# Pairing the row maxima of two PSUM banks on VectorE, spreading the value products, and weighing one chunk earlier, in a two-layer decoder

## What is computed

```python
qh  = (q @ w_q).reshape(B, L, 16, 8).transpose(0, 2, 1, 3)   # 16 heads of 8
kvp = c @ w_kv                                   # c: 6404 context rows
k, v = kvp[..., :8], kvp[..., 8:]                # one key and value head for all
prob = softmax(einsum('bhid,bjd->bhij', qh, k) / sqrt(8))
out  = einsum('bhij,bjd->bhid', prob, v)...reshape(B, L, 128) @ w_concat
```

## Time and profile before

| | before |
|---|---|
| median of 3 runs | 2091.1 us |
| the profiled execution, its own time | 2089.03 us |
| its span | 2087.3 us |
| PE busy | 1963.3 us (94%) |
| DVE busy | 1571.0 us (75%) |
| ACT busy | 1360.1 us (65%) |
| POOL busy | 98.9 us (5%) |
| maxima of the first cross attention, L981 | 1664 reductions, 976.3 us busy |
| exponentials there, L965 | 1632 activations, 874.0 us busy |

### The profile page before, as it was taken

How to read it: one execution, slowest core, us unless ns; L and a number is a source line. 1 busy time by engine, 2 the same in 40 slices (tenths; PEclk the granted TensorE clock), 3 DMA queues, 4 the chain that set the end, 5 groups by cost and what they waited for, 6 DMA issues and landing times. The chain is left out here.

```text
span 2087.3 us, 38311 instructions
## 1 busy us (share of the span) xinstructions
PE 1963.3 (94%) x15036; PEld 1030.1 (49%) x15036; DVE 1571.0 (75%) x3006; ACT 1360.1 (65%) x2404; POOL 98.9 (5%) x84
## 2 busy tenths in 40 slices
PE   7778999999999999999999999898999988999898
PEld 2225744444444444444444444676344435777755
DVE  7995899999999999999999951333788854444344
ACT  5333488888888888888888887332588863333421
POOL 1660000000000000000000000001000000000000
PEclk8998899999999999999999999898999998999999
DMA  4210000000000000000000000110000000000011
GB/s 144 71 61 0 1 2 2 2 1 2 2 1 2 2 1 2 2 2 1 2 2 1 2 1 1 31 38 18 0 1 1 2 1 1 1 1 0 11 33 28
DMA packets 22853, 24.73 MB, mean 12 GB/s; under 512 B 5712, under 2 KB 20080, under 8 KB 22432
## 3 DMA queue, kind: packets, MB, share of 16 engines
q1 hardware_dynamic: 21504, 20.37, 3.3%
q10 hardware_dynamic: 1184, 2.10, 0.3%
HBM read 21.74 MB, written 0.59 MB: 11 GB/s over the span
## 5 line engine op out<-in xcount | busy, mean ns | idle before, releaser
L981 DVE TENSOR_REDUCE sb_max_partial<-ps_max_ps 128x1 f32<-128x512 f32 (+1 forms) x1664 | 976.3, 662 | 61.1 <-PE ps_max_ps L796 60.4
L965 ACT ACTIVATE sb_probs<-ps_score_ps 128x512 f32<-128x512 f32 (+1 forms) x1632 | 874.0, 597 | 111.0 <-PE ps_score_ps L929 65.6
L929 PE MATMUL ps_score_ps<-sb_q_stack,sb_key_stack 64*128 64x512 f32 x1632 | 586.6, 444 | 3.9 <-ACT sb_probs L965 3.4
L796 PE MATMUL ps_max_ps<-sb_key_stack,sb_q_stack 64*128 64x512 f32 (+1 forms) x1560 | 555.7, 438 | 0.0
L918 PE MATMUL ps_acc_ps<-sb_probs,sb_val_ones 128*32 128x256 f32 x6528 | 465.0, 387 | 0.2 <-ACT sb_probs L965 0.2
L929 PEld LDWEIGHTS ps_score_ps<-sb_q_stack,sb_key_stack 64*128 64x128 f32 x1632 | 276.8, 184 | 326.2 <-ACT sb_probs L965 267.9
L796 PEld LDWEIGHTS ps_max_ps<-sb_key_stack,sb_q_stack 64*128 64x128 f32 x1560 | 265.1, 184 | 9.6 <-DVE sb_max_partial L981 7.3
L918 PEld LDWEIGHTS ps_acc_ps<-sb_probs,sb_val_ones 128*32 128x32 f32 x6528 | 156.4, 108 | 207.0 <-issue 144.2
L1630 DVE TENSOR_REDUCE sb_s_max_partial<-ps_s_ps 128x1 f32<-128x512 f32 x256 | 159.9, 683 | 21.7 <-PE ps_s_ps L1539 21.6
L1617 ACT ACTIVATE sb_s_probs<-ps_s_ps 128x512 f32<-128x512 f32 x256 | 140.7, 597 | 25.6 <-PE ps_s_ps L1567 16.6
L1914 DVE TENSOR_SCALAR_CACHE_REDUCE sb_x_scores<-ps_x_score_ps 128x1024 f32<-128x1024 f32 (+1 forms) x56 | 62.1, 1111 | 82.4 <-PE ps_x_score_ps L1855 82.4
(11 more groups left out here) (269 smaller groups left out, 1827.7 us busy)
## 6 DMA issues: line engine op xcount, KB each, us to landing
sb_val<-c_rows SPq DMA_DIRECT2D x16, 512.0 KB, 3.7
sb_e_w<-L_ffn_rW SPq DMA_DIRECT2D x30, 128.0 KB, 2.1
sb_e_w<-L_ffn_W_T SPq DMA_DIRECT2D x24, 128.0 KB, 2.1
sb_ctx_T<-ctx_T SPq DMA_DIRECT2D x1, 1664.0 KB, 7.7
sb_ctx_T<-ctx_T ACTq DMA_DIRECT2D x1, 1538.0 KB, 8.7
sb_x_T<-x_T SPq DMA_DIRECT2D x1, 512.0 KB, 3.8
sb_x_tok<-x ACTq DMA_DIRECT2D x1, 512.0 KB, 11.1
sb_e_w<-L_ffn_sW SPq DMA_DIRECT2D x4, 128.0 KB, 2.4
```

Of the source, the lines that this page charges most:

```text
L796: nc.tensor.matmul(bank((blk, u))[:, 0:n], queries, keys, start=True, stop=True).then_inc(tile_ready, 1)
L929: nc.tensor.matmul(score_ps[:, e % 3, :], k.key_stack[rows(blk), c * P:(c + 1) * P], q_stack[rows(blk), blk // 2, j * HALF:(j + 1) * HALF] ...
L965: nc.scalar.activation(probs[0:n, c % 3, j * HALF:(j + 1) * HALF], score_ps[0:n, e % 3, :], ACT.Exp).then_inc(exp_done, 1)
L981: nc.vector.tensor_reduce(partial[:, blk % 2, h, r:r + 1], bank((blk, u))[:, 0:RANGES[r][1]], AX.X, ALU.max).then_inc(tile_used, 1)
```

## The change

There are four parts.

1. **Pairs.** Where two tiles that follow one another lie in the first and second bank of the ring (and both are full 512-key tiles of one head), VectorE reduces both with one instruction over 2 x 512 columns, `pair_maxima` (L998 of the changed kernel). It waits for the second tile, and frees both banks when it ends. All other tiles keep their own reduction.
2. **Values.** The 51 value products of layer 0 are no longer jobs. They are issued one at a time between the tiles of block 0, from tile 21 to tile 96, all into one PSUM bank, and ScalarE copies them at the end with two instructions in place of five. 27 jobs are left, spread over the same tiles. The queries of the upper half use one PSUM bank in place of two, and each waits for the one before.
3. **Chunk 49** (`NCH - 2`) is weighed at the end of its own block, ahead of the transposes of shift B, no longer behind score 0 of the next block. Chunk 50 stays behind score 0.
4. **Self attention.** Likewise chunk 6 (`NT - 2`) is weighed at its block's end, and chunk 7 behind score 1 of the next block in place of score 0; ScalarE copies the sum after exponential 1 in place of 0.

```diff
-            val0_jobs = [(c, min(13, NCH - 1 - c)) for c in range(0, NCH - 1, 13)] + [(NCH - 1, 1)]
...
+            def paired(blk, u):
+                return (u % NR < NR - 2 and place[(blk, u)] % PLACES in (0,)
+                        and place[(blk, u + 1)] == place[(blk, u)] + 1)
...
-                return score_ps[:, i % 2, :]
+                return score_ps[:, 0, :]
...
-                    pe.wait_ge(q_done, i - 3 if i < HB else i - 1)
+                    pe.wait_ge(q_done, i - 3 if i < HB else i)
...
+            def value(pe, c):
+
+                n = P if c < NCH - 1 else TAIL
+                ins = nc.tensor.matmul(v_ps[0:n, c, :], k.ctx_T[:, c * P:c * P + n], k.w_kv[:, HD:2 * HD], start=True,
+                                       stop=True)
+                if c == NCH - 1:
+                    ins.then_inc(v_ready, 1)
...
+            VALUE_AT = {FIRST_JOB + 1 + 3 * c // 2: c for c in range(NCH)}
...
                     if e == 0 and blk > 0:
-                        weigh(pe, blk - 1, NCH - 2)
                         weigh(pe, blk - 1, NCH - 1)
...
+                weigh(pe, blk, NCH - 2)
                 if blk + 1 < NB:
                     issue(pe, (blk + 1, "B"))
...
+            def pair_maxima(dve, blk, u):
+
+                h, r, at = u // NR, u % NR, place[(blk, u)] % PLACES
+                dve.wait_ge(tile_ready, blk * TILES + u + 2)
+                nc.vector.tensor_reduce(partial[:, blk % 2, h, r:r + 2], max_ps[:, at:at + 2, :],
+                                        AX.X, ALU.max).then_inc(tile_used, 2)
...
                         for u in range(TILES):
-                            maximum(dve, blk, u)
+                            if u > 0 and paired(blk, u - 1):
+                                pair_maxima(dve, blk, u - 1)
+                            elif not paired(blk, u):
+                                maximum(dve, blk, u)
...
-                    if e == 0 and blk > 0:
-                        weigh(pe, blk - 1, NT - 2)
+                    if e == 1 and blk > 0:
                         weigh(pe, blk - 1, NT - 1)
...
+                weigh(pe, blk, NT - 2)
```

More of the change, by code:

```diff
@@ L725, in context_attention @@
             job_ready, job_copied = k.sem("layer1_job_ready"), k.sem("layer1_job_copied")
+            v_ready, v_taken = k.sem("ctx_v_ready"), k.sem("ctx_v_taken")
             EXPS = NCH * JOBS
-            val0_jobs = [(c, min(13, NCH - 1 - c)) for c in range(0, NCH - 1, 13)] + [(NCH - 1, 1)]
             key_jobs = [(c0, min(HALF, CTX - c0)) for c0 in range(0, CTX, HALF)]
             val_jobs = [(c, min(4, NCH - 1 - c)) for c in range(0, NCH - 1, 4)] + [(NCH - 1, 1)]
-            VAL0, KEYS = len(val0_jobs), len(key_jobs)
-            NJOBS = VAL0 + KEYS + len(val_jobs)
+            KEYS = len(key_jobs)
+            NJOBS = KEYS + len(val_jobs)
             EARLY_JOBS = NJOBS
@@ L853, in job_bank, with take_values @@
                 return acc_ps[:] if i % 2 else score_ps[:, 2, :]
-            def layer1_job(pe, i, to):
[L857 to L864, removed]
+            v_ps = score_ps[:, 1, 0:NCH * HD].rearrange("p (c e) -> p c e", e=HD)
+            def value(pe, c):
[4 more added lines that the diff above has]
+                    ins.then_inc(v_ready, 1)
+            def take_values(act):
+                act.wait_ge(v_ready, 1)
+                nc.scalar.copy(k.val_ones[:, 0:NCH - 1, 0:HD], v_ps[:, 0:NCH - 1, :])
+                nc.scalar.copy(k.val_ones[0:TAIL, NCH - 1, 0:HD], v_ps[0:TAIL, NCH - 1, :]).then_inc(v_taken, 1)
+            def layer1_job(pe, i, to):
+                if i < KEYS:
+                    c0, cols = key_jobs[i]
                     ins = nc.tensor.matmul(to[:, 0:cols], k.wk1[:], k.ctx_T[:, c0:c0 + cols], start=True, stop=True)
                 else:
-                    c, m = val_jobs[i - VAL0 - KEYS]
+                    c, m = val_jobs[i - KEYS]
                     n = P if c < NCH - 1 else TAIL
@@ L1013, in _ @@
                             subtract_high(pe, MINUS_AT[u])
+                        if u in VALUE_AT:
+                            value(pe, VALUE_AT[u])
                         for i in jobs_at(u):
@@ L1025, in _ @@
                     pe.wait_ge(job_copied, EARLY_JOBS)
+                    pe.wait_ge(v_taken, 1)
                     for blk in range(NB):
                         attend(pe, blk)
-                    for v in range(NCH - 2, NCH):
-                        weigh(pe, NB - 1, v)
+                    weigh(pe, NB - 1, NCH - 1)
                 @block.scalar
@@ L1045, in _ @@
                             copy_job(act, i, job_bank(i))
+                        if VALUE_AT.get(u) == NCH - 1:
+                            take_values(act)
                         if u == FIRST_TURN:
@@ L1715, in _ @@
                         attend(pe, blk)
-                    for v in range(NT - 2, NT):
-                        weigh(pe, NB - 1, v)
+                    weigh(pe, NB - 1, NT - 1)
                 @block.scalar
```

## The result

The changed kernel took 2153.7 us (median of 4 runs, 2152.0 to 2155.4) against 2092.4 us before: a ratio of 1.029, 95% interval 1.027 to 1.032. That is 61 us slower, where I had forecast 16 and a range that ended at 2132.

The account below looks back on a forecast made before the run. A loop of ScalarE and TensorE, not VectorE, bounds the blocks. 2089.0 - 10.3 (values) - 4.1 (chunk 49) + 32 (pairs) = 2106.6, plus 2.1 against the median: about 2108 us, range 2070 to 2132.

Parts of the forecast that it names:

- The term for the pairs: Cross attention blocks 1 to 15: pairs freeing the first bank late cost 5.3 + 15.0 + 11.8 = 32 us.
- the late pairs: Blocks 1 to 15: pairs starting at scores e % 6 = 2, 3 or 4 end after their first bank is needed; 32 us.
- Pair by pair, end against need: One regular period: each pair's end compared with when its first bank is needed; three kinds late by 0.22 to 0.32 us.
- s3+s4: Blocks 1 to 15, 53 pairs at scores e % 6 = 3, 4: late by 0.22 us, cost 53 x 0.10 = 5.3 us.
- s4+s5: Blocks 1 to 15, 68 pairs at scores e % 6 = 4, 5: late by 0.22 us, cost 15.0 us.
- s2+s3: Blocks 1 to 15, 59 pairs at scores e % 6 = 2, next 3: late by 0.32 us, cost 11.8 us.
- The 0.12 us that I let s1 and s0 absorb: Scores e % 6 = 1 and 0: TensorE absorbs up to 0.12 us of a tile's lateness there.
- In time: Pairs starting at scores e % 6 = 5, 0 or 1 return the first bank by its need, so no cost.
- s1+s2: Blocks 1 to 15, 45 pairs at scores e % 6 = 1, 2: end 4.18 against need 4.16 us, no cost.
- s0+s1: Blocks 1 to 15, 59 pairs at scores e % 6 = 0, 1: end 3.58 against need 3.93 us, no cost.
- The lead-in: Block 0: its 23 pairs cost nothing, the first bank being asked for 1.8 us after the second tile is issued.
- lateness feeds on itself: Rival, blocks 1 to 15: lateness carries over through lengthening periods, pairs cost 50 us, 2127 us; chance 0.13.

Follow-up runs that it names:

- 0.13 us of reserve a tile: Against the changed kernel with every tile reduced singly (2078.1 us): single maxima take 384 of 512 columns; 2063.2 us, with pairs 2129.4 us.
- The kernel with s2+s3 alone: Changed kernel keeping only the 59 pairs of the tiles of scores e % 6 = 2 and next 3: 2103.5 us.

## Why the prediction was wrong

**The direction and its cause were right.** The blocks' pace is a loop of ScalarE and TensorE, and pairs buy nothing on a VectorE that isn't the pace. They hand back the first bank too late. The pair's 1.22 us, the 0.065 us that it saves (from 662.12 to the next reduction at 663.26 are 1.14 us, two single ones take 1.20), and the longer period where a pair ends late are all as read from the rows. One thing has to be added: with 0.13 us of reserve a tile VectorE gains 14.9 us, so it does hold some bursts of a block.

The Trainium skill ("Perfetto Trace Analysis", "Optimizing Scalar/DVE Operations") says that where an engine isn't saturated but causes bubbles on others, smaller instructions can let work finish sooner. The runs agree with that: the kernel without pairs is 75.6 us faster. Its sentence that grouping can help a saturated engine gave no gain here, though VectorE was busy for 930 of 964 us.

**The term for the pairs was mis-sized: 32 us, measured 75.6.** To see where, I split the time between the blocks' scores in the traces with and without pairs (per block; a burst is counted from its first score to the weighing behind it, at shift A and the border to the next burst):

| | without pairs | with pairs | difference x 15 |
|---|---|---|---|
| bursts ahead of two chunks | 17.11 us | 19.78 us | 40 us |
| bursts ahead of one chunk | 14.33 us | 15.20 us | 13 us |
| the two bursts at shift A | 4.45 us | 5.35 us | 13 us |
| the border | 4.45 us | 4.86 us | 6 us |

With 3.3 us more in the lead-in (84.2 against 80.9) that is 76. My 32 us stood for the late pairs alone, which by themselves cost 62. What I missed:

- *The step "Pair by pair, end against need": the ends were too early.* Without the irregular places the holds were 0.32 us for s3+s4, 0.27 for s4+s5 and 0.45 for s2+s3, not 0.22, 0.22 and 0.32. A bank is handed over 0.05 us after the reduction ends, which I left out. A pair for which VectorE stood still also begins 0.07 us later than I took it: 0.63 us after s3's tile is issued in all 59 pairs s2+s3, and 0.53 in place of 0.46 behind s4's. The 0.12 us that I let s1 and s0 absorb did show: with holds of 0.32 and 0.45 the stretch grew by 0.21 and 0.33.
- *One period, VectorE at its emptiest.* I took a period in which VectorE starts s3's tile as soon as it is usable. The trace of before has it 0.12 us behind on average at that tile, and 0.25 or more in a quarter of the periods. The 23 dear pairs s4+s5 (0.53 to 0.78 us) lie where it is behind already.
- *"In time" without a margin.* I called s1+s2 in time with its end 0.02 us after its need. All 45 such pairs hold s5's tile, by 0.21 us on average. The pairs with a real margin, s0+s1, cost nearly nothing.
- *Places outside the regular period.* I priced every pair by the regular period, also at shift A, at the border and where two tiles follow one score. The kernel with s2+s3 alone shows what that left out: its 36 pairs in regular places cost some 11 us (0.33 a pair in their own burst, where I had 0.20), the 15 around shift A 9 us and the 8 at the border 6 us. That the first figure is near the 11.8 forecast for all 59 is chance.
- *The lead-in.* I put its 23 pairs at nothing; they cost about 2 us. The other 1.3 of the 3.3 us is the clock: the changed kernel's lead-in has its first 6.2 us at the lower level, the one without pairs 3.2. The kernels with no pair in block 0 take 80.8 and 80.9 us with the short stretch and 82.1 to 82.3 with the long one, and with reserve, both short, pairs add 2.1 (82.0 against 79.9).

The rival "lateness feeds on itself" (50 us) was nearest by size and isn't the cause: the kinds of pairs add up, and reserve takes away only 9 us.

**The values: -10.3 forecast, -10.2 measured** without pairs (91.1 to 80.9 us). In the kernel without pairs the clock is at 1.00 but for the first 3.2 us, which were at the lower level before too:

```profile
178.60:199.00 20.40, 19.49 (x58) 10.88 (x59) 14.25 (x24) 11.63 (x19) 3.24 (x9) 0.92 0.00 1
199.00:259.50 60.50, 60.01 (x339) 46.05 (x339) 50.07 (x88) 24.53 (x45) 0.00 (x0) 1.00 0.00 1
```

The agreement to 0.1 us is partly luck, since that first stretch alone moves the lead-in by 1.3 us from kernel to kernel. No run changes the values alone; jobs and queries moved with them. The Trainium skill ("Perfetto Trace Analysis", "Matmul Optimizations") advises back-to-back batches, which would have made this 0. With products of 8 columns the batches are where the clock fell, and without them it stayed.

**Chunk 49: -4.1 forecast, about -6 measured** (0.39 us a block, from 64.28 to 63.89). ScalarE's timeline at a border, without pairs:

```profile
1154.16 0.60 ACT L975 ACTIVATE sb_probs<-ps_score_ps 128x512 f32<-128x512 f32 x1
...
1154.66 0.37 ACT L965 COPY sb_gathered<-ps_acc_ps 128x256 f32<-128x256 f32 x1
...
1154.99 2.56 ACT L975 ACTIVATE sb_probs<-ps_score_ps 128x512 f32<-128x512 f32 x5
```

Exponential 1 begins 0.83 us after exponential 0; before, it was 1.26. I had added the durations 0.60 and 0.37, but here the copy starts 0.10 us before the exponential ends, and the next exponential 0.04 before the copy ends.

**The self attention: 0 forecast, 1.6 us slower.** As reasoned, a wait was exchanged for another. The copy's 7.0 us are gone, and in the waits after the change, 1565 to 1772 us, stands the line below. Before, this wait was 1.4 us, once.

```profile
ACT sb_s_q_stack L1632 <- PE ps_s_ps L1572: 11.7, 16, 1.8
```

## What to carry to other kernels

An instruction that does two tiles' work waits for the second and holds the first tile's buffer twice as long. With a ring of four banks in a tight loop that cost up to 0.43 us a pair (mean of one kind), and 0.065 was saved. Before grouping on an engine that isn't the pace, take the time from the second input's arrival to the first buffer's next use, and want a margin: 0.35 us sufficed here in the regular period, and an end 0.02 us past the need did not. When pricing this from a trace, take the state the engine is usually in, not its emptiest period, and go through the irregular places (borders, turns, two tiles behind one score) one by one.

## What I had not expected

- Giving VectorE 0.13 us of reserve a tile, with nothing else changed, gained 14.9 us in a kernel where TensorE waits for it only 7.5 us in all. Those waits lie at fixed places on the loop: s2's tile is held 0.24 us in the 13th burst of each block, 0.13 in the 19th and 0.35 in the 23rd, where two tiles follow one score. With reserve these bursts are shorter by 5, 2 and 5 us in all, and the border by 2.
- TensorE's clock fell to the lower level during runs of 8-column products while PE was busy for all of the 24 us of that window. With the same products laid singly between tiles it stayed at 1.00.
